# A wide cross attention with its steps in an alternating order, its value projections two tiles to a bank, and an expert routing with another sort and search

## The reference

```python
# stage 2, routing: scores (2048 tokens, 64 experts) are sorted for each expert; groups of
# 64 ranks are summed; the 512 best groups of all experts are kept, the other scores are 0
router_scores = softmax(xt @ Wr + br)                       # (2048, 64)
sorted_vals = take_along_axis(router_scores, argsort(-router_scores, axis=0), axis=0)
group_score = sorted_vals.reshape(32, 64, 64).sum(axis=1)   # 32 groups for each expert
_, top_flat = top_k(group_score.reshape(-1), 512)
# stage 4, wide attention: 8 sequences, 16 heads of 64, 256 queries, 1601 + 1 keys
q = heads(x @ Wq) * 64 ** -0.5                              # (8, 16, 256, 64)
k, v = split(context @ Wkv)                                 # context is (8, 1601, 256)
k, v = with_null(heads(k)), with_null(heads(v))             # 1602 keys
out = softmax(q @ k.T) @ v                                  # then @ Wout, and a norm
```

## Time and profile before

| | |
|---|---|
| runs | 4994.01, 5001.19, 4988.22 us; median 4994.01 |
| profiled execution | 4985.95 us |
| its span, first to last instruction | 4984.1 us |
| mean granted TensorE clock | 0.89 of full speed |
| stage 2, routing up to the end of its threshold | 344 to 502 us in the span |
| stage 4, first to last scores copy | 807.0 to 2575.5 us in the span |

### The profile page before, as it was taken

One profiled execution on the slowest core, in us unless ns is written; L12 is line 12 of the kernel. 1 busy time (PEld: TensorE's weight loads), 2 busy tenths in 40 slices (PEclk: granted clock), 3 DMA queues, 4 the chain that ended last, 5 costly groups with the idle time before them and its releaser, 6 DMA issues. The chain is left out here.

```text
span 4984.1 us, 77257 instructions
## 1 busy us (share of the span) xinstructions
PE 4023.9 (81%) x29194; PEld 2215.1 (44%) x29259; DVE 3487.3 (70%) x5453; ACT 2467.5 (50%) x3477; POOL 1335.3 (27%) x984
## 2 busy tenths in 40 slices
PE   5640787999999999999986995866996677888883
PEld 3630345666666666666653332432443342222231
DVE  6569554777777777777774445766774558888868
ACT  2120224666666666666652223543664354777772
POOL 0000001656666665666675203000000100000000
PEclk5565898999999999999997996987997688999996
DMA  0010510000000000000004106315650333323200
GB/s 19 1 53 0 105 60 27 1 14 14 1 14 1 14 1 14 1 14 1 1 1 154 37 0 152 54 15 102 86 80 4 91 59 64 56 49 56 49 2 9
DMA packets 145927, 184.01 MB, mean 37 GB/s; under 512 B 21562, under 2 KB 110156, under 8 KB 144932
## 3 DMA queue, kind: packets, MB, share of 16 engines
q1 hardware_dynamic: 137860, 162.65, 15.8%
q0 software_dynamic: 6528, 16.42, 1.4%
q10 hardware_dynamic: 1184, 0.12, 0.0%
HBM read 141.04 MB, written 35.08 MB: 35 GB/s over the span
## 5 line engine op out<-in xcount | busy, mean ns | idle before, releaser
L2993 POOL TENSOR_TENSOR arena<-arena 128x512 f32<-128x512 f32 (+1 forms) x768 | 1132.7, 1477 | 692.0 <-ACT arena L2949 638.7
L2444 ACT ACTIVATE arena<-ps 128x1024 f32<-128x1024 f32 (+1 forms) x688 | 703.9, 1024 | 313.1 <-PE ps L2369 302.6
L2462 DVE TENSOR_REDUCE arena<-ps 128x2 f32<-128x826 f32 (+1 forms) x576 | 564.7, 980 | 165.9 <-PE ps L2315 157.5
L3009 DVE TENSOR_TENSOR arena<-arena 128x1024 f32<-128x1024 f32 (+1 forms) x448 | 646.6, 1482 | 13.9 <-ACT arena L2976 13.9
L3031 DVE TENSOR_TENSOR arena<-ps,arena 128x512 f32<-128x512 f32 (+1 forms) x768 | 530.1, 690 | 177.3 <-ACT arena L2943 144.3
L2315 PE MATMUL ps<-arena 48*128 48x413 bf16 (+3 forms) x1920 | 431.3, 330 | 130.2 <-DVE arena L2462 65.7
L2943 ACT ACTIVATE arena<-ps 128x1024 f32<-128x1024 f32 (+1 forms) x448 | 410.5, 960 | 205.2 <-PE ps L2871 193.5
L2855 PE MATMUL ps<-arena 128*128 128x256 f32 (+1 forms) x1664 | 444.0, 392 | 20.6 <-DVE arena L3017 19.3
L2949 ACT ACTIVATE arena<-arena 128x1024 f32<-128x1024 f32 (+1 forms) x448 | 424.9, 992 | 50.8 <-DVE arena L3009 48.3
L2388 PE MATMUL ps<-arena 128*9 128x256 f32 (+2 forms) x5504 | 430.7, 384 | 11.4 <-ACT arena L2432 8.5
L2871 PE MATMUL ps<-arena 64*128 64x256 f32 (+1 forms) x3328 | 427.6, 391 | 5.6 <-ACT arena L2965 1.3
(11 more groups left out here) (637 smaller groups left out, 5710.1 us busy)
## 6 DMA issues: line engine op xcount, KB each, us to landing
arena<-ctx_parts SPq DMA_DIRECT2D x96, 200.1 KB
arena<-ctx_parts SPq DMA_DIRECT2D x192, 100.1 KB
arena<-fs_rows SPq DMA_DIRECT2D x128, 128.0 KB, 4.1
arena<-in_ctx_feat SPq DMA_DIRECT2D x8, 1601.0 KB, 6.4
arena<-in_ctx SPq DMA_DIRECT2D x16, 768.0 KB
arena<-diff_att_stack SPq DMA_DIRECT2D x60, 192.0 KB
ctx_parts<-arena SPq DMA_DIRECT2D x24, 400.2 KB, 3.5
arena<-in_w SPq DMA_DIRECT2D x1, 6416.0 KB, 18.4
```

Source lines behind the costliest of these rows:

```text
L2444: act.activation(self.prob[0:rows, u % 3, :], self.ps[0:rows, 2 * (u % 2):2 * (u % 2) + 2, :].rearrange("p n c -> p (n c)"), ACT.Exp).then ...
L2462: ins = dve.tensor_reduce(dst[:, :, j // 2], self.ps[:, 4:6, 0:hi - lo], AX.X, ALU.max)
L2993: pool.tensor_tensor(acc[0:rows, u % 2, :], before, sc[0:rows, u % 2, t, :], ALU.add).then_inc(added, 1)
L3009: dve.tensor_tensor(e, e, mb[0:rows, u % 2, None, :].to_broadcast([rows, n, 2 * S]), ALU.subtract).then_inc(sub_done, 1)
```

## The change

Three things change in stage 4 and three in stage 2.

1. Steps alternate between two orders. Every second one (`values_first`) has values, scores, ring on PE; the others have ring, scores, values. So ring stands next to ring, and values next to values.
2. On ACT a values-first step has both exponentials, then the copies of the scores, then the ring's copies. The other kind has the first exponential, the ring's first copy, the second exponential, the ring's other copies, and the copies of the scores last. On DVE the maxima stay last in either kind; a `turn` is reduced behind both subtractions or between them.
3. A ring product `v` is two key tiles in one bank (512 columns), with one copy; `q` comes last in its step. Two units have 7 such products, and 13 before.
4. The sort's steps are all of two instructions of 512 elements: the first step of each merge reads its partner in reverse (`mirrored`), so that all pairs go the same way.
5. After the halves are crossed, 4 steps stand where 10 were; a minimum for each group is taken by a reduction (`low`).
6. The count above a sum is taken 5 times, as a search by halves over a row's 16 sums, each with three or four small instructions that wait for one another; a fill of `fs` moves up ahead of the wait for PE's spread.

```diff
@@ expert_scores
-            def compare(k, j, both):
+            def compare(j, mirrored):
...
+                v = lambda t, side: t[:, :].rearrange("p (n s j) -> p n s j", s=2, j=j)[:, :, side, :]
+                other = lambda side: v(a, side)[:, :, ::-1] if mirrored else v(a, side)
+                tt(v(b, 0), v(a, 0), other(1), ALU.max)
+                link(tt(v(b, 1), v(a, 1), other(0), ALU.min))
...
-            while j >= 1:
-                compare(HALF, j, False)
+            while j >= GR:
+                compare(j, False)
...
+            part, size, r = gs[:, :], NG, 0
+            while size >= 1:
+                half = size // 2
+                at = max(half - 1, 0)
+                probe = part[:, at:at + 1]
+                link(ts(above[:, :], ps[:, 0:4, :].rearrange("p n c -> p (n c)"), probe, 0.0, ALU.is_gt, ALU.add,
+                        accum_out=small[:, 0, r:r + 1]))
+                dve.tensor_copy(small[:, 7, r:r + 1], probe)
+                if half:
+                    link(ts(cols[:, 7:8], small[:, 0, r:r + 1], float(BUDGET), -BIG, ALU.is_lt, ALU.mult))
+                    nxt = small[:, 6 - r % 2, 0:half]
+                    link(stt(out=nxt, in0=part[:, 0:half], scalar=cols[:, 7:8], in1=part[:, half:size], op0=ALU.add,
+                             op1=ALU.max))
@@ WideSlots.ring_of
-        return turn + keys[0:2] + bcast + keys[2:] + late
+        return turn + values + keys[0:1] + bcast + keys[1:] + late
@@ stage4, tensor
             for s in range(plan.first, plan.end, 2):
+                if plan.values_first(s):
+                    for slot in plan.pair(s, plan.LAG):
+                        values(*slot)
+                else:
+                    ring(s)
                 for slot in plan.pair(s):
                     scores(*slot)
+                if plan.values_first(s):
+                    ring(s)
+                else:
+                    for slot in plan.pair(s, plan.LAG):
+                        values(*slot)
@@ stage4, scalar
+                if plan.values_first(s):
+                    exponentials(s, slice(0, 2))
+                    copy_scores(s)
+                    copy_ring(s, slice(0, None))
+                else:
+                    exponentials(s, slice(0, 1))
+                    copy_ring(s, slice(0, 1))
+                    exponentials(s, slice(1, 2))
+                    copy_ring(s, slice(1, None))
+                    copy_scores(s)
@@ stage4, vector
+                if plan.values_first(s):
+                    subtract(s, slice(0, 2))
+                    turned(s)
+                else:
+                    subtract(s, slice(0, 1))
+                    turned(s)
+                    subtract(s, slice(1, 2))
                 for x, u, k in plan.pair(s):
                     dve.wait_ge(s_copied, x + 1)
```

More of the change, by code:

```diff
@@ L1018, in expert_scores @@
         diag = st.sb("diag", [P, NG, P])
-        above = [st.sb(f"above{k}", [P, NG * P]) for k in range(2)]
+        above = st.sb("above", [P, NG * P])
+        low = st.sb("low", [P, NG])
         small = st.sb("small", [P, 8, NG])
@@ L1144, in _ @@
                ALU.mult).then_inc(s["diag_ready"], 1)
+            dve.tensor_reduce(low[:, :], ranked, AX.X, ALU.min)
+            dve.memset(e["fs"][:, :], 1.0)
             dve.wait_ge(s["spread_ready"], 1)
[L1146 to L1151, removed]
@@ L2747, in ring_of @@
     def ring_of(self, s):
-        turn, keys, bcast, late = [], [], [], []
+        turn, values, keys, bcast, late = [], [], [], [], []
+        if 0 <= s < self.SLOTS:
+            values.append(("v", s // 14, s % 14 // 2))
         for x in (s, s + 1):
@@ L2892, in _, with ring @@
             pe.wait_ge(ones_ready, 1)
-            for s in range(plan.first, plan.end, 2):
-                for slot in plan.pair(s):
-                    scores(*slot)
-                for slot in plan.pair(s, plan.LAG):
-                    values(*slot)
+            def ring(s):
                 for key in plan.ring_of(s):
@@ L2922, in _ @@
                         ins.then_inc(ring_ready, 1)
+            for s in range(plan.first, plan.end, 2):
+                if plan.values_first(s):
[3 more added lines that the diff above has]
+                    ring(s)
+                for slot in plan.pair(s):
+                    scores(*slot)
+                if plan.values_first(s):
[3 more added lines that the diff above has]
+                        values(*slot)
                 for u in plan.ended(s, plan.LAG + 2):
@@ L2932, in _, with copy_scores @@
             act.wait_ge(null_moved, 32)
-            for s in range(plan.first, plan.end, 2):
+            def copy_scores(s):
                 for x, u, k in plan.pair(s):
@@ L3001, in _, with subtract @@
             ins.then_inc(null_k_ready, 1)
-            for s in range(plan.first, plan.end, 2):
-                for x, u, k in plan.pair(s, plan.LAG - 2):
+            def subtract(s, part):
+                for x, u, k in plan.pair(s, plan.LAG - 2)[part]:
                     n = len(plan.tiles_of(k))
```

74 lines of the change are left out of this document (35 added, 39 removed).

## The result

The changed kernel takes 5110.59 us (median of four runs, 5109.25 to 5120.63), the kernel before 4991.11 beside it: ratio 1.0243, interval 1.0219 to 1.0266. Forecast were 5088 and slower. The profiled execution took 5109.45 us, its span is 5107.6. First the page's part 1, then the stretch of the earlier trace rows.

A forecast was written before the change was run, and what follows sets the result against it. PE was taken to bound stage 4 now, a closed DVE-ACT chain after the change. The profiled 4985.95 us, less 40 for routing, plus 134 for stage 4, gave 5080; the runs' median 5088, range 5040 to 5140 (8 in 10: 4965 to 5160).

The forecast's parts named there:

- The marks that were named: Signs in stages 2 and 4: stage 1880 to 1920 us, PE below 285, DVE's wait 450, ACT's 300, subtractions 550, counts 5.
- rival 1: Stage 4: PE stays the bound and drains less, gaining 38 to 144 us; 4916 down to 4810; chance 0.10.
- rival 2: Stage 4: the chain binds and PE is never late, 10 to 19 us more; 4969; chance 0.10.
- rival 3: Stage 4: subtractions meet additions as often as now, 99 us more; 5187; chance 0.10.
- rival 4: Stage 2: routing gives nothing, as reversed reads and chained search eat it; 5088 + 10 to 40; chance 0.04.
- the sum: Stage 4: the chain's 111.3 us plus PE's lateness 8.0, over two, makes 59.6 for 14 slots.
- surcharges: PE late in some ring-first steps, through `turn`, ring copies or being two products behind: 8.0 us in 28 slots.
- +134: Stage 4: 4.2 us more than now for 14 slots, x 32, makes 134 us more.
- Subtractions: Stage 4, DVE: each priced at 1.26 us, meeting no POOL addition; at the present mean 99 us more.
- Routing: Stage 2, serial chain on DVE: sort 7.0, steps after the crossing 8.0, counts 22.5, fill 2.2; 39.7 us less.
- the 38 priced: Stage 4, PE: two array-shape changes of six fewer in two steps, 1.2 us for 14 slots, 38 us for the stage.

The follow-up runs named there:

- values next to values: New ring in the old order, but every second step does values ahead of scores on PE, rings apart: 4938.13 us, ratio 0.9890 to the kernel before.
- one exponential last: Changed kernel; ACT copies scores first in values-first steps, and in ring-first steps takes one exponential, ring's copies, scores' copies, second exponential: 5000.49 us, ratio 0.9998.
- the new ring in the old order: Changed kernel with scores, values, ring in every step as before, on PE, ACT and DVE; new routing kept: 4895.93 us, ratio 0.9792 to the kernel before.
- The chain alone: New ring and routing in the old order, with ACT's exponentials ahead of the copies of scores in every step: 4939.08 us, ratio 0.9888 to the kernel before.

## Why the prediction was right

**The mechanism** was the one forecast: ACT's order closes a chain, PE falls out of the bound. The marks that were named are there, or close by: PE at 273.6 of 300 us (below 285), the stage at 1922 (2 above its range), DVE's and ACT's idle times above 450 and 300, subtractions at 514 us with a mean of 1.182 (for 550 and 1.25, marks that left out the short slots), counts in five. Rivals 1 and 2 fall with these idle times and the stage, rival 3 with the subtractions, rival 4 with the routing. The forecast of 5088 is 0.4% below the median.

**The chain's size.** On DVE's timeline the same subtraction, the first of the ring-first step with a `turn` and `q`, comes back every 28 slots:

```profile
1301.60 1.22 DVE L3046 TENSOR_TENSOR arena<-arena 128x1024 f32<-128x1024 f32 x1
...
1321.12 0.43 DVE L3085 COPY branch<-ps 128x256 f32<-128x256 f32 x1 [2.53 <-PE ps L2927]
...
1425.06 1.22 DVE L3046 TENSOR_TENSOR arena<-arena 128x1024 f32<-128x1024 f32 x1
...
1543.97 1.22 DVE L3046 TENSOR_TENSOR arena<-arena 128x1024 f32<-128x1024 f32 x1
```

The second cycle lasts 118.91 us (1425.06 to 1543.97), 59.5 for 14 slots, and 59.6 was the sum. It holds by kind of step too, once surcharges, reciprocals and short slots are put to the steps in which they stand. A plain values-first step is 7.24 for 7.4, and all seven are 52.4 for 53.2. Steps that begin with `turn` are 10.21 and 10.81 for 10.2 and 10.6, the other ring-first steps 8.77 to 9.48 for 8.3 to 9.4, and all seven are 66.5 for 66.1. No step is off by more than 0.6, and part of that cancels.

**What was missing in it.** The first cycle lasts 123.46. Its difference is two waits that the sum did not have. One is the output projection, in every second cycle (eight times): DVE copies its product ahead of the subtractions (L3085) and waits 2.53 for PE, and the step at 1311.81 is 9.66 where its like at 1435.27 is 6.70. So 8 x 2.96 = 24 us. The other is the clock: the step at 1339.27 is 12.40 where its like at 1459.77 is 10.81, since `k` behind a wait of 2.37 ran at the lower level, 1.2 GHz, for part of the time (granted clock 0.71 in that stretch, and 2.58 us for 1.58). That is 1.6 in eight of the steps, 13 us. In the place of `turn` at 1299.62 the clock falls too, but there `k` at 1303.47 still waits 0.31 for the reduction, so that little of it counts. The first ten slots, which have no subtraction, last 31.6 for 42.5, 11 less, and the plain cycle's 59.5 for 59.6 is some 5 less. 1902 + 24 + 13 - 11 - 5 is 1923, and 1922 was measured: **+153.5 for +134**, the term of the sum that was mis-sized.

**Subtractions** were priced alone, and seem to have met few additions: 1.182 in the mean, 1.482 before. The Trainium skill (SBUF — State Buffer, "SBUF: two separate sides") has DVE's operations with two inputs in SBUF and GpSimd's that read SBUF hold their shared port exclusively, and the traces agree, since the means of both go up and down together: here POOL's additions take 1.298, before 1.477, and with values next to values subtractions take 1.669 and additions 1.551.

**Routing** gave 38.9 for 39.7 up to the scan behind it (476.49 for 515.08, the stage having begun 0.33 later): the sort 6.8, the steps after the crossing 8.0, the counts 22.4 (14.1 from 452.13 to 466.20), and 2.3 behind them, where the fill was. A round is 2.91, as priced. The fill and the reduction for `low` cost 0.6 where they stand now: from the end of the product that PE spreads to the first count it is 6.1 us (446.03 to 452.13), and it was 5.5.

**What the prediction did not see** is that its three parts of stage 4 have opposite signs. Two `v` tiles to a bank, and `q` late, were priced at nothing in the forecast (rival 1 gave the ring's waits at most 3.3 us for 14 slots); they are worth 61 us in the old order, 1.9 for 14 slots. PE's idle time ahead of `v` and `k` falls there from 23.4 us to 0.0, and its busy time at them from 844.5 to 794.1. The alternating order costs 1922.0 - 1707.6 = 214 us against the same ring in the old order. So -36 for routing, -61 for the ring and +214 for the order make +117, where 119 were measured. The forecast was not helped by this: it adds up the chain's own time, which the old ring's waits don't enter. And the first rival's gain can be seen, though buried: with two changes of array shape fewer, PE's busy time is 418.7 us for 427.4 at scores, and 398.6 for 412.7 at values (one exponential last against the new ring in the old order), 23 of the 38 priced, as far as modelled ends tell.

**The 214 us.** Opening the chain on ACT gives back 94 to 109 of them (49 where both exponentials stand last in ring-first steps); some 106 stay in the alternating order with the best ACT order tried. They are seen as waits of PE inside the ring, and putting `v` ahead of `turn` only moved these. The chain alone costs 37 in the old order and values next to values 40; the parts don't add up to 214, and why they cost more together is not shown. How much of the 106 is the uneven spacing of scores, and how much the rings next to each other, stays open: no order of ACT without either chain or waits was found. The unchanged rest behind the stage was 7.3 us longer in this execution, 5.5 longer in the new ring's; that is not explained and within what executions differ.

## What to carry to other kernels

Before an engine's instructions are put in another order, write down for each engine what every instruction waits for, and look for a circle in which each link stands, in program order, behind one that waits for the link before: its length is then a bound, however idle the engines are. Doubling one link and comparing with the same doubling in the old order (113 us against 39 here) tells cheaply whether it is on such a circle. And time the parts of a change apart: here the ring's part, worth -61 us, and the order's, worth +214, came as one.

## What the runs showed of the hardware

- An operation of DVE with two inputs of 512 elements, one of them read in reverse group by group, took as long as one with forward reads: 0.69 us each, and 1.33 for a step of either kind.
- TensorE's granted clock fell to its lower level in the changed kernel after waits of PE of 2.1 to 2.4 us, not after each: at 1341.13 a `k` behind a wait of 2.37 took 2.58, at 1461.73 one behind 2.46 took 1.58. From 800 to 2700 us the mean granted clock was 0.98; with `v` ahead of `turn`, and waits of 3.15, it was 0.96; with the new ring in the old order, from 800 to 2470, 1.00.
